# Attention on one core: the next row's first two words between the last squares, and the weighted sum one row later

## The reference

```python
attn = jnp.einsum('bhnd,bhmd->bhnm', q, k) * attn_scale
attn, a_scale = fq_act(attn)
attn = log_int_softmax(attn, a_scale)
out = jnp.einsum('bhnm,bhmd->bhnd', attn, v)

def log_int_softmax(x, sf, bits=BITS_S):
    x_int = x / sf
    x_int = x_int - x_int.max(axis=-1, keepdims=True)
    exp_int, _ = _int_exp(x_int, sf)      # 2**(n - octave) * ((r + b/2)**2 + c)
    exp_sum = exp_int.sum(axis=-1, keepdims=True)
    softmax_out = jnp.round(exp_sum / exp_int)
    rounds = round_ln(softmax_out)        # nearest power of two
    return jnp.where(rounds >= 2.0 ** bits, 0.0, 2.0 ** (-qlog))
```

## Time and profile before

| | |
|---|---|
| median of the runs | 1019.19 us (3 runs, 1018.41 to 1020.95) |
| the profiled execution | 1023.18 us, span 1021.4 us |
| DVE busy in the span | 873.0 us (85%) |
| ACT busy | 708.9 us (69%) |
| PE busy, PE weight load | 705.7 us (69%), 483.7 us (47%) |
| POOL busy | 168.2 us (16%) |

### The profile page before, as it was taken

One profiled execution on the slowest core, in us unless ns is written; L12 is line 12 of the kernel. 1 busy time (PEld: TensorE's weight loads), 2 busy tenths in 40 slices (PEclk: granted clock), 3 DMA queues, 4 the chain that ended last, 5 costly groups with the idle time before them and its releaser, 6 DMA issues. The chain is left out here.

```text
span 1021.4 us, 23392 instructions
## 1 busy us (share of the span) xinstructions
PE 705.7 (69%) x6531; PEld 483.7 (47%) x6532; DVE 873.0 (85%) x2391; ACT 708.9 (69%) x1374; POOL 168.2 (16%) x276
## 2 busy tenths in 40 slices
PE   3783387757788376676767667666644386999997
PEld 3562144425555234343434334333323254998996
DVE  5879997988888889999999999999978874676766
ACT  0345365977888789988988998999845293554553
POOL 5851220017664100000000000000004530000000
PEclk9986598988999777878877887788757597999999
DMA  8000000001111111111111111111022004455452
GB/s 260 3 3 0 0 1 1 1 1 40 37 37 37 40 31 25 24 24 24 25 24 24 24 26 24 24 25 24 17 91 75 17 1 155 147 194 193 171 194 82
DMA packets 84274, 54.75 MB, mean 54 GB/s; under 512 B 53704, under 2 KB 83176, under 8 KB 83976
## 3 DMA queue, kind: packets, MB, share of 16 engines
q1 hardware_dynamic: 83208, 54.11, 17.4%
q0 software_dynamic: 1024, 0.13, 0.3%
HBM read 11.90 MB, written 3.76 MB: 15 GB/s over the span
## 5 line engine op out<-in xcount | busy, mean ns | idle before, releaser
L1377 DVE SCALAR_TENSOR_TENSOR expo<-expo,con,pow 128x153 f32<-128x153 f32 x480 | 146.2, 377 | 0.7 <-ACT expo L1287 0.7
L1287 ACT ACTIVATE expo<-at_rem,con 128x459 f32<-128x459 f32 x160 | 98.1, 644 | 14.7 <-PE at_rem L1160 11.2
L962 DVE TENSOR_REDUCE rs_ends<-rs_banks 128x770 f32 (+1 forms) x96 | 89.3, 957 | 12.8 <-PE rs_banks L934 10.6
L784 PE MATMUL at_banks<-pick,row_top 128*128 128x459 bf16 x160 | 73.5, 459 | 37.7 <-ACT word L1250 37.1
L1413 DVE CUSTOM_DVE_ANT_0 weight_top<-weight_top,line 128x2448 uint16<-128x2448 uint16 x64 | 85.6, 1351 | 8.1 <-ACT line L1279 6.3
L1159 PE MATMUL at_rem<-word,ident_half 128*128 128x459 f16 x160 | 64.7, 404 | 37.2 <-ACT expo L1287 34.6
L883 ACT ACTIVATE rs_banks<-rs_banks 128x770 f32<-128x770 f32 x96 | 74.6, 796 | 22.4 <-PE rs_banks L926 21.6
L1243 ACT ACTIVATE pT_all<-at_pT 128x768 bf16<-128x768 int16 (+3 forms) x160 | 79.0, 563 | 13.8 <-PE at_pT L1183 8.3
L1250 ACT ACTIVATE word<-at_banks 128x459 uint8<-128x459 f32 x160 | 79.9, 562 | 9.9 <-PE at_banks L789 8.7
L1943 ACT ACTIVATE qk<-e_p,b1s 128x153 f32<-128x153 f32 x192 | 58.9, 392 | 29.0 <-PE e_p L1904 27.8
L1904 PE MATMUL e_p<-X,qk 128*128 (+1 forms) x960 | 72.9, 236 | 7.7 <-DMA qk<-vt 6.9
(11 more groups left out here) (389 smaller groups left out, 2036.2 us busy)
## 6 DMA issues: line engine op xcount, KB each, us to landing
qk<-vt SPq DMA_DIRECT2D x64, 384.0 KB, 3.1
rs_kb<-qk SPq DMA_DIRECT2D x128, 28.7 KB, 2.0
kb<-qk SPq DMA_DIRECT2D x128, 28.7 KB
patches<-in_patches SPq DMA_DIRECT2D x4, 768.0 KB
vi<-vt SPq DMA_DIRECT2D x32, 96.0 KB, 2.0
out<-vi SPq DMA_DIRECT2D x32, 96.0 KB, 1.8
pj_w<-in_w SPq DMA_DIRECT2D x1, 2304.0 KB, 8.3
qb<-qk SPq DMA_DIRECT2D x128, 6.0 KB
```

The lines of the kernel that those rows point to most:

```text
L784: pe.matmul(bank[:, 0:3 * N], top, pick[:, 3 * i:3 * i + 3, :].rearrange("p w n -> p (w n)"), start=True, stop=False, skip_group_check=True)
L962: v.tensor_reduce(ends[:, :, n, 5 * b:5 * b + 5], banks[:, slot(u, b), :, 0:5 * W].rearrange("p i (t n) -> p i t n", n=W), AX, ALU.max).th ...
L1287: act.activation(bank(ex, b), rem[:, (u + b) % 2, 0:3 * N], ACT.Square, scale=2.0 ** 24, bias=c(5)).then_inc(sq_done, 1)
L1377: ins = v.scalar_tensor_tensor(ex[:, t, :], ex[:, t, :], c(7), pw[:, t, :].bitcast(BF16), ALU.add, ALU.mult, accum_out=tot[:, t:t + 1])
```

## The change

It moves instructions, and adds and removes none of the arithmetic.

On ScalarE words 0 and 1 of row m+1 are written in step m: between the third and fourth square, and between the fourth and fifth. The step then opens with words 2 to 4 alone. Each word now waits for the product of its own bank that reads the old word (`rem_done`), in place of one wait ahead of the five. Words 0 and 1 of row 0 stand ahead of the loop.

On TensorE the weighted sum is that of m-3 in place of m-2, and stands behind scores 3 and 4 of row m, ahead of the transposes. The five remainders follow one another. The last row's weighted sum stands behind the loop.

```diff
                 def body(i, kk):                                  # TensorE
-                    now, last, nxt = batch(i, kk, 0), batch(i, kk, 2), batch(i, kk, -1)
+                    now, last, gone, nxt = batch(i, kk, 0), batch(i, kk, 2), batch(i, kk, 3), batch(i, kk, -1)
                     if now is not None:
                         n, u, half = now
                         scores(n, u, half, range(3, NB))
+                    if gone is not None:
+                        weighted(*gone)
...
                     if now is not None:
-                        remainder(n, u, range(2))
-                    if last is not None:
-                        weighted(*last)
-                    if now is not None:
-                        remainder(n, u, range(2, NB))
+                        remainder(n, u, range(NB))
...
                 steps(pe, body)
+                weighted(B - 1, 1, B // 2 - 1)
...
-                def distances(n):
-                    if not first(n, 1):
-                        act.wait_ge(rem_done, n * NB)
-                    for b in range(NB):
+                def distances(n, which):
+                    for b in which:
+                        if not first(n, 1):
+                            act.wait_ge(rem_done, n * NB - NB + b + 1)
                         act.wait_ge(s.scored, n * NB + b + 1)
...
+                    nxt = batch(i, kk, -1)
                     if now is not None:
-                        distances(now[0])
+                        distances(now[0], range(2, NB))
...
-                    for h, which in enumerate(((0,), (1, 2, 3, 4))):
+                    for h in range(2):
                         if mid is not None:
                             line_of(mid[0], h)
                         if now is not None:
-                            squares(now[0], now[1], which)
+                            squares(now[0], now[1], ((0,), (1, 2))[h])
+                    for b in range(2):
+                        if nxt is not None:
+                            distances(nxt[0], (b,))
+                        if now is not None:
+                            squares(now[0], now[1], (3 + b,))
```

More of the change, by code:

```diff
@@ L1317, in _ @@
                 act.wait_ge(set_up, 3)
+                distances(0, range(2))
                 steps(act, body)
```

## The result

The changed kernel runs in 1009.98 us (median of 4 runs, 1007.16 to 1012.25) against 1019.35 us (4 runs, 1018.41 to 1020.95): a ratio of 0.990, 95% interval 0.988 to 0.993, 9.4 us or 0.9% faster. The forecast was 1009.2 us and 10.0 us of gain.

The account below looks back on a forecast made before the run. VectorE nearly bounds the loop, losing 0.35 us a step to ScalarE's late lines. 28 x (12.36 - 12.04) = 9.0 us plus 1.0 for the first steps gives 1019.2 - 10.0 = 1009.2 us, range 1006 to 1016.

Parts of the forecast that it names:

- The floor: VectorE's packed step in the loop: 12.01 us with its work unchanged, against a mean of 12.36, so 0.35 a step winnable.
- The tolerance: What ScalarE can lose in a step before VectorE stands: 0.27 + 0.53 + 0.42 = 1.2 us.
- Squares: ScalarE's squares, waiting for remainders: give back 0.45 us at half clock, 0.23 in any step; idle time under 4 us.
- Words: ScalarE's words, waiting for scores: all 7.7 us of idle time ahead of them taken as gone.
- ScalarE's waits: ScalarE's idle time ahead of squares, ranks and words: all waits for TensorE, 27.9 us or 1.0 a step.
- The moved sum: TensorE's weighted sum between scores and transposes: ranks lose 0.8 us at half clock, bounds 0.5 to 1.2, none at full.
- third group: Third group of TensorE's transposes, ahead of ranks: its wait stays, 0.35 us a step on average, 0.77 at worst.
- First steps: Waits for the line outside the 28-step stretch: a further gain of 1.0 us, bounds 0 and 2.4.
- SyncE's queue: Next row's load, queued behind values awaiting the sum: starts 2.3 us later, cover 3.8 us, costs nothing.
- The sum in the way: Rival: the weighted sum ahead of the transposes eats much of the gain; step 12.27, 1015.7 us; chance 0.16.
- Stalls off the path: Rival: only VectorE's own waits, 3.9 us, can be won; gain 3 us or less, 1016.5 to 1019; chance 0.10.
- The lower clock: Rival: TensorE's clock stays at 0.50 after a longer gap; step 12.71, 9.8 us slower, 1029.0 us; chance 0.08.

Follow-up runs that it names:

- e3: The changed kernel with two more shares on ScalarE, 0.62 us a step, written to a tile nobody reads: step 12.49 us, median 1024.1 us.
- e1: The kernel before with ScalarE's half of the change alone (early words), TensorE's order as before: step 12.00 us, median 1009.8 us, ratio 0.9895.
- e2: The kernel before with TensorE's half of the change alone (moved weighted sum), ScalarE's order as before: step 13.50 us, median 1052.3 us.
- e9: ScalarE's half alone, VectorE's extremes left out, with both lines in a row ahead of square 0: step 11.79 us, median 1001.9 us.

## Why the prediction was right, and where it was off

**The floor.** VectorE's packed step of 12.01 us and the 0.35 us above it were read correctly; 28 steps gave 9.5 us in the trace, 9.0 forecast.

**The tolerance.** 1.2 us a step from two waits and a margin. It gave 0.8 us over the floor for the worst step before; the longest in the stretch is 12.75, 0.74 over. The forecast was that the change uses 1.1 of it at half clock. e3 bears it out in kind: with 0.62 us more some steps stay at 12.01, so there is a tolerance, and others don't. In size it was somewhat off: the mean of 12.49 is at the upper edge of the 12.3 to 12.5 expected, and the long steps reach 12.81, 0.8 over the floor where 0.5 was expected.

**Squares.** Expected under 4 us idle, measured 3.9. **Words.** Expected none, measured 0.0. **ScalarE's waits.** The 27.9 us that the prediction put down to TensorE are all idle time ahead of the three groups; by the releasers in the earlier trace rows 7.4 + 6.5 + 7.7 = 21.6 us of them are waits for TensorE. No term of the sum rests on the difference. ScalarE's wait for VectorE ahead of the line was expected in most steps and stands in 15 of 28.

**The moved sum.** The new wait was put at 0.8 us at half clock, bounds 0.5 to 1.2; the timeline has up to 1.07, and 10.6 + 2.8 us in all. The rest of the ranks' wait was taken as unchanged (9.7 us, third group) and it went: the wait for L1183 was 6.5 us and is 0.4 after. e1, where the sum hasn't moved, has 1.7, so most of this comes with the early words. In the changed kernel the clock is also mostly back by the time the third group comes (0.91 from 527.8 to 529.2 us), perhaps because the ranks start later. The total of 14.8 is less than the sum I allowed for.

**First steps.** 1.0 us taken, bounds 0 to 2.4; three steps fell from 33.3 to 30.8, by 2.5. Of this 1.4 us is the first step, 8.44 before and 7.07 after, and that part is not shown to be the change's. e2, which keeps the words in their old place, has 7.11 there, and the granted clock tells the two apart; before, then e2, from the first octave to the second (the clock is the third number from the end, 0.65 and 1.00):

```profile
354.20:362.60 8.40, 5.80 (x25) 2.48 (x26) 6.36 (x34) 5.56 (x10) 0.00 (x0) 0.65 0.14 32
355.10:362.30 7.20, 4.40 (x34) 2.08 (x34) 6.40 (x35) 5.29 (x11) 0.00 (x0) 1.00 0.16 37
```

The other two steps fell by 1.1, about what was taken. In the profiled pair the attention is 12.3 us shorter, in the medians the whole kernel 9.4. Whether the profiled execution's 4.0 us over the other runs were stall, the question that the prediction left open, stays open: no run here separates these parts.

**SyncE's queue.** The load now starts 1.5 us behind the values that wait for the sum:

```profile
526.81 0.59 SPq L1100 DMA_DIRECT2D vi<-vt  x1
...
528.30 0.69 SPq L772 DMA_DIRECT2D kb<-qk  x1
...
534.41 0.89 SPq L1106 DMA_DIRECT2D row_top<-top_rows  x1
```

With 2.0 us to landing it is there at 536.4, and TensorE starts on that row at 539.11: cover 2.7 us, 3.8 forecast. It cost nothing: no DMA stands among TensorE's waits above.

**The rivals.** The sum in the way: right in mechanism, as e2 and e3 show, and too small with the words early to move the step. Stalls off the path: out, since the step fell to the floor. (Its price, a gain of 3 us, makes 1016.2 us and not 1016.5.) The lower clock: the granted clock fell from 0.81 to 0.79, not below 0.7. TensorE's longest wait of a step was forecast at about 3 us and lasts 2.27 to 2.94, in all 28 steps, where before none was longer than 2.42. So the mechanism is there, and its price is small. e1, with the sum back in that wait, has no wait over 2.42 us and a granted clock of 0.85. The Trainium skill, TensorE: Matmul & The Clock Gate, section HAM oscillation, states that waits between bursts of matmuls bring the lower clock back, and the trace agrees with it in direction: 0.79 without the sum in the longest wait, 0.85 with it. Here that was worth nothing, since ScalarE had room enough.

**What I did not see.** That the whole gain is ScalarE's half, and that the ring of 11.96 us lay under the floor. The prediction priced the moved sum as a cost alone, 0.8 us at half clock, and didn't go on to say that the early words without it would do as well. The second could have been found by adding up a ring instead of one engine's work. Neither changed the forecast, as 12.01 is above 11.96.

## What to carry to other kernels

When a loop runs near one engine's packed step, the question for an edit is how late the other engines may be before that engine waits: read the waits that the second engine spends on the first in a packed step, add them, and compare with what the edit costs and gives back. Test the halves of such a change apart, and with a small load added: two kernels of equal time can differ by half a microsecond a step in room, and the one with room is the one that takes the next step. And before work is taken from the bounding engine, add up the ring through its neighbours; here the first 0.05 us of relief was all that paid until the order inside the ring was changed (e9, 11.79 in place of 11.96).

## What was not expected of the hardware

Leaving out up to 0.54 us of VectorE's work a step won 0.05 us, with both engines showing idle time and none of them full. And the granted clock of the loop is 0.79 in the change and 0.85 in e1, with the same work in the same time: the two differ by the place of the weighted sum's 15 products alone. That is one profiled execution each. Over the whole span the four runs of each kernel have 0.845 to 0.850 and 0.852 to 0.861, so the direction holds and its size may be smaller.
